# Two attention units a step: stacked queries, scores as 64-row products on both row tiles, low value products a step late

## The reference, cut to what matters

```python
x = x + tanh(g_xattn[0]) * attention(layernorm(x), ctx, ctx, 0, mask)   # the stage that changes
x = x + tanh(g_ffn[0]) * ffn(layernorm(x), ...)                          # unchanged here
# attention, f32: b=8, s=224, t=750, g=8 key/value heads, r=4 query heads each, d=64
scores = einsum('bsgrd,btgd->bgrst', xq, xk) / sqrt(64) + mask
probs  = softmax(scores, axis=-1)
out    = einsum('bgrst,btgd->bsgrd', probs, xv)
```

## Time and profile before

| what | value |
|---|---|
| time, median of 3 runs | 1172.92 us (1172.48 to 1173.42) |
| time of the profiled execution | 1173.51 us |
| its span, first to last instruction | 1171.7 us |
| granted TensorE clock | 1.00 of full speed throughout |
| first to last copy of transposed units (L742) | 20.3 to 879.9 us |
| busy PE, DVE, ACT, POOL | 1108.0, 1017.9, 897.6, 871.9 us |

### The profile page before, as it was taken

The page is one execution under the profiler, slowest core; times in us unless marked ns, Lnnn a source line. Parts: engine busy times, 40 slices in busy tenths (PEclk is TensorE's granted clock), DMA queues, the critical chain, the costliest instruction groups (busy, mean ns, idle before and its releaser), DMA issues.

```text
span 1171.7 us, 40472 instructions
## 1 busy us (share of the span) xinstructions
PE 1108.0 (95%) x17123; PEld 842.1 (72%) x17380; DVE 1017.9 (87%) x2325; ACT 897.6 (77%) x1162; POOL 871.9 (74%) x760
## 2 busy tenths in 40 slices
PE   4999999999999999999999999999999999999998
PEld 3777777777777777777777777777776655555554
DVE  6999999999999999999999999999984899676776
ACT  4898888888888888888888888888882443655544
POOL 6899999999988988898898889888892111333424
PEclk9999999999999999999999999999999999999999
DMA  9521331233114212412331132122126600002214
GB/s 327 153 70 42 67 115 43 54 77 98 42 49 111 77 42 60 114 49 55 70 105 42 48 72 54 42 60 51 49 81 188 239 1 1 1 36 109 102 79 180
DMA packets 102580, 95.44 MB, mean 81 GB/s; under 512 B 84481, under 2 KB 85505, under 8 KB 98562
## 3 DMA queue, kind: packets, MB, share of 16 engines
q1 hardware_dynamic: 101682, 91.79, 27.1%
q10 hardware_dynamic: 720, 1.05, 0.2%
HBM read 71.75 MB, written 20.97 MB: 79 GB/s over the span
## 4 chain that ended last, share of the span: by engine, by line
PE 79%; DVE 10%; issue 4%; POOL 3%; DMA 2%; ACT 1%; SPq 1%; DVEq 0%; POOLq 0%
PE psum L924 22%; PE psum L937 16%; PE psum L983 11%; PE psum L960 6%; PE psum L954 6%; PE psum L955 6%; DVE arena L1313 5%; DVE arena L1354 3%; PE psum L1061 3%; PE psum L902 2%; PE psum L970 2%; POOL arena L586 1%; PE psum L1100 1%; DMA arena<-in_k_t 1%; PE psum L996 1%
## 5 line engine op out<-in xcount | busy, mean ns | idle before, releaser
L586 POOL TENSOR_TENSOR arena<-arena 128x768 bf16<-128x768 f32 x448 | 651.2, 1470 | 72.6 <-ACT arena L742 71.6
L1313 DVE CUSTOM_DVE_ANT_0 arena<-psum,arena 128x750 f32<-128x750 f32 x448 | 419.3, 936 | 53.0 <-PE psum L924 45.9
L742 ACT ACTIVATE arena<-psum 128x768 f32<-128x768 f32 x448 | 362.9, 810 | 103.6 <-PE psum L937 103.5
L746 ACT ACTIVATE arena<-arena,neg_max 128x750 f32<-128x750 f32 x448 | 409.6, 914 | 4.2 <-DVE neg_max L1313 4.0
L924 PE MATMUL psum<-arena 128*128 128x238 bf16 (+1 forms) x1570 | 317.5, 318 | 38.6 <-issue 32.5
L937 PE MATMUL psum<-ident,arena 64*128 64x64 f32 x5376 | 263.5, 231 | 3.2 <-ACT arena L742 2.0
L924 PEld LDWEIGHTS psum<-arena 128*128 128x128 bf16 x1792 | 137.4, 97 | 144.4 <-issue 1.7
L937 PEld LDWEIGHTS psum<-ident,arena 64*128 64x128 f32 x5376 | 203.7, 138 | 38.8 <-issue 8.4
L954 PE MATMUL psum<-arena 128*128 128x65 bf16 (+1 forms) x2688 | 227.8, 195 | 0.0
L955 PE MATMUL psum<-arena 128*128 128x64 bf16 (+1 forms) x2688 | 226.7, 193 | 0.0
L954 PEld LDWEIGHTS psum<-arena 128*128 128x128 bf16 (+1 forms) x2688 | 198.6, 98 | 4.9 <-DVE arena L1354 0.2
(11 more groups left out here) (167 smaller groups left out, 1001.3 us busy)
## 6 DMA issues: line engine op xcount, KB each, us to landing
arena<-in_k_t SPq DMA_DIRECT2D x128, 187.5 KB, 3.2
arena<-in_v_rows SPq DMA_DIRECT2D x64, 192.0 KB, 2.9
out<-arena SPq DMA_DIRECT2D x10, 1024.0 KB, 3.9
arena<-in_x_top SPq DMA_DIRECT2D x8, 1024.0 KB, 5.3
arena<-in_x_rest SPq DMA_DIRECT2D x8, 768.0 KB, 4.6
spill<-arena SPq DMA_DIRECT2D x96, 64.0 KB, 2.3
arena<-spill SPq DMA_DIRECT2D x6, 1024.0 KB, 10.2
arena<-in_w_t SPq DMA_DIRECT2D x4, 1024.0 KB, 16.3
```

What stands on the lines that cost most here:

```text
L586: pool.tensor_tensor(p_lo[:, n % RING, :], p_sb[:, n % RING, :], high(p_sb[:, n % RING, :]), ALU.subtract).then_inc(p_split, 1)
L742: act.activation(p_sb[:, n % RING, :].rearrange("p (c h q) -> p h c q", h=2, q=HALF), turned_ps, ACT.Copy).then_inc(evac_a, 1)
L746: act.activation(s_sb[:, n % RING, 0:CTX], s_sb[:, n % RING, 0:CTX], ACT.Exp, bias=neg_max[:, n % 4, :], scale=-1.0).then_inc(exped, 1)
L1313: dve.tensor_tensor_reduce(s_sb[:, n % RING, 0:CTX], flat_ps[:, score_at(n):score_at(n) + CTX], mask_sb[:, max(n % UNITS - REP + 1, 0), :] ...
```

## The change

The kernel after works on two consecutive units in one step; a pair of groups (14 units) is 7 steps, and there are 224 steps.

- Scores: the stationary operands are `q_hi` and `q_lo`, with 64 rows for the first unit of the step and 64 for the second. Each matmul has 64 contraction rows, on row tile 0 for the first unit and on row tile 1 for the second, and the two are issued one behind the other. There are three products (high-high, low-high, high-low) in place of four. Both units of the step write banks 0 to 3, and the next step's scores wait until both were reduced.
- The units of the second group of a pair come in the order `SECOND`, so that the two units of a step always lie in the two row halves of one turned block.
- Low values move from DVE to POOL (`split_v`). The low probabilities of both units are one POOL instruction. The low value products of a step are issued in the next step.
- Queries: one high and one low instruction over 128 partitions in place of two each over 64.
- DVE does the two reductions of a step first and then the rest of that step; ACT does copy, exponential, copy, exponential.
- Rings of four; SP's list goes by pairs of groups: its order around `spill_rest` and the second `load_k` is new. The load of `wvu` now waits for the last scores.

```diff
-RING = 3
+RING = 4
...
+SECOND = (4, 0, 1, 2, 3, 5, 6)
...
+            for both in range(PAIRS):
+                b, at = both // 4, both % 4
+                if both + 1 < PAIRS:
+                    sp.wait_ge(scored, 2 * UNITS * both + UNITS + 1)
+                    load_k(2 * both + 2)
+                if both > 0:
+                    sp.wait_ge(valued, 2 * UNITS * both)
+                    load_v(2 * both + 1)
+                if at == 0 and b > 0:
                     spill_rest(b - 1)
...
+                if at == 0 and b + 1 < BATCH:
                     gather_rest(b + 1)
...
+                if at == 0 and b + 2 < BATCH:
+                    load_top(b + 2)
+                if both + 1 < PAIRS:
+                    sp.wait_ge(scored, 2 * UNITS * (both + 1))
+                    load_k(2 * both + 3)
...
+                if both + 1 < PAIRS:
+                    sp.wait_ge(valued, 2 * UNITS * both + UNITS)
+                    load_v(2 * both + 2)
...
+            for i in range(FIRST, NP):
+                both, p = place(i)
+                j = i + 1
+                if 0 <= j < NP:
+                    pool.wait_ge(evac_a, 2 * j + 2)
+                    if j >= 2:
+                        pool.wait_ge(valued, 2 * (j - 1))
+                    slots = slice(2 * j % RING, 2 * j % RING + 2)
+                    pool.tensor_tensor(p_lo[:, slots, :], p_sb[:, slots, :], high(p_sb[:, slots, :]), ALU.subtract).then_inc(p_split, 1)
...
+                if p == 1:
+                    split_v(2 * both + 1)
+                if both + 1 < PAIRS:
+                    if p == 1:
+                        split_k(2 * both + 2)
+                    if p == 4:
+                        split_k(2 * both + 3)
+                    if p == 5:
+                        split_v(2 * both + 2)
...
+            def copy_unit(n):
+                act.wait_ge(turned, n + 1)
+                if n >= RING and n % 2 == 0:
+                    act.wait_ge(p_split, n // 2 - 1)
...
+            for i in range(FIRST, NP):
+                both, p = place(i)
+                for s in range(2):
+                    if 0 <= i + 1 < NP:
+                        copy_unit(2 * (i + 1) + s)
+                    if 0 <= i + 2 < NP:
+                        exp_unit(2 * (i + 2) + s)
...
+                if both >= 0 and p == 4 and both + 2 < PAIRS:
+                    norm_top(both + 2)
+                later = both // 4 + 1
+                if both >= 0 and both % 4 == 3 and later < BATCH:
+                    if p == 0:
+                        norm_rest(later, 0)
+                        norm_rest(later, 1)
+                    if p == 1:
+                        norm_rest(later, 2)
...
+            def score_pair(j):
...
+                if j >= 1:
+                    pe.wait_ge(maxed, 2 * j)
                 for cols in (slice(0, MAIN), slice(MAIN, CTX)):
...
+                    for term in range(3):
+                        for s in range(2):
+                            rows = slice(HALF * s, HALF * s + HALF)
+                            u = groups[s] % 2
+                            q = q_lo if term == 1 else q_hi
+                            kk = k_lo[rows, u, cols] if term == 2 else high(k_raw[rows, u, cols])
+                            mm = pe.matmul(flat_ps[:, score_at(s) + cols.start:score_at(s) + cols.stop], q[rows, both % 2, p, :], kk,
+                                           start=(term == 0), stop=(term == 2))
+                mm.then_inc(scored, 2)
...
+            for i in range(FIRST, NP + 1):
+                both, p = place(i)
+                if 0 <= i + 1 < NP:
+                    turn_unit(2 * (i + 1))
+                if 0 <= i + 3 < NP:
+                    score_pair(i + 3)
+                if 0 <= i + 1 < NP:
+                    turn_unit(2 * (i + 1) + 1)
...
+                if i >= 1:
+                    value_low(i - 1)
+                if 0 <= i < NP:
+                    value_high(i)
...
+                if 0 <= both and both + 1 < PAIRS:
+                    if p == 2:
+                        turn_q(both + 1, 0)
+                    if p == 6:
+                        turn_q(both + 1, 1)
...
+                        if s == 1 and n >= RING:
+                            dve.wait_ge(turned, n - RING + 1)
+                        dve.tensor_tensor_reduce(s_sb[:, n % RING, 0:CTX], flat_ps[:, score_at(s):score_at(s) + CTX],
...
+                if both >= 1 and p == 0:
+                    add_part(2 * both - 1, range(0, 3) if both < PAIRS else range(UNITS))
+                if both >= 1 and p == 1:
+                    add_part(2 * both - 1, range(3, UNITS))
+                if p == 4:
+                    add_part(2 * both, range(0, 3))
+                if p == 5:
+                    add_part(2 * both, range(3, UNITS))
+                if both + 1 < PAIRS:
+                    if p == 2:
+                        split_q(both + 1, 0)
+                    if p == 6:
+                        split_q(both + 1, 1)
...
+                if p == 3 and both % 4 == 1 and both // 4 + 1 < BATCH:
+                    merge_top(both // 4 + 1)
+                    merge_rest(both // 4 + 1)
```

More of the change, by code:

```diff
@@ L336, in flamingo_block, with place, unit, part_turns @@
         block = ctx.enter_context(nc.Block())
[L338 to L353, removed]
-        FIRST_BANK = (1, 0, 1)
[L356 to L364, removed]
+        def place(i):
+            return divmod(i, UNITS)
+        def unit(n):
+            both, at = divmod(n, 2 * UNITS)
+            return (2 * both, at) if at < UNITS else (2 * both + 1, SECOND[at - UNITS])
+        FIRST_TURNS = (range(0, 2), range(2, 4), range(4, 7))
+        FIRST_BANK = (1, 0, 1)
+        def part_turns(part):
+            return range(0, 4) if part == 0 else range(4, 7)
+        def part_bank(part):
+            return 1 - part
+        def parts_split(both, part):
+            return 2 * both + 2 + part
+        ALL_PARTS = parts_split(PAIRS - 1, 1)
         def rows_of(t):
@@ L602, in _ @@
-                if window == GROUPS - 2 and m == 4:
+                if both < 0:
+                    continue
+                if p == 1:
[7 more added lines that the diff above has]
+                        split_v(2 * both + 2)
+                if both % 4 == 2 and both // 4 + 1 < BATCH:
+                    if p == 0:
+                        root(both // 4 + 2, whole)
+                    if p == 1:
+                        factors(both // 4 + 2, whole)
@@ L893, in turn_rows @@
[L893 to L901 removed]
+                    pe.wait_ge(rest_widened, NB)
@@ new lines, in value_high @@
+            def value_high(j):
+                for s in range(2):
+                    n = 2 * j + s
+                    g, m = unit(n)
+                    u = g % 2
+                    if n % UNITS == 0:
+                        pe.wait_ge(v_split, g + 1)
+                        if g >= 2:
+                            pe.wait_ge(x_added, g - 1)
+                        pe.wait_ge(q_split, min(g + 3, ALL_PARTS) if g else 2)
+                    pe.wait_ge(evac_a, n + 1)
+                    at = m * (D + 1)
+                    o = mix_ps[:, u, at:at + D + 1]
+                    fresh = s == 0 or n % UNITS == 0
+                    for c in range(NCH):
+                        rows = chunk_rows(c)
+                        hi = high(p_sb[0:rows, n % RING, c * 128:(c + 1) * 128])
+                        pe.matmul(o, hi, high(v_raw[0:rows, u, c, :]), start=(fresh and c == 0), stop=False, skip_group_check=True)
+                        pe.matmul(o[:, 0:D], hi, v_lo[0:rows, u, c, :], start=False, stop=False, skip_group_check=True)
@@ new lines, in value_low @@
+            def value_low(j):
+                pe.wait_ge(p_split, j + 1)
+                for s in range(2):
+                    n = 2 * j + s
+                    g, m = unit(n)
+                    at = m * (D + 1)
+                    for c in range(NCH):
+                        rows = chunk_rows(c)
+                        lo = p_lo[0:rows, n % RING, c * 128:(c + 1) * 128]
+                        mm = pe.matmul(mix_ps[:, g % 2, at:at + D + 1], lo, high(v_raw[0:rows, g % 2, c, :]), start=False, stop=(c == NCH - 1),
+                                       skip_group_check=True)
+                    mm.then_inc(valued, 1)
```

396 lines of the change are left out of this document (147 added, 249 removed).

## The result

The kernel after takes 1234.53 us (median of 4, 1229.31 to 1235.78), the kernel before 1173.17 on the same chip (1172.48 to 1173.70): a ratio of 1.052 [1.048, 1.055], so 5% slower. The prediction was 1144 (1106 to 1178), faster with a chance of 0.79. It was wrong, in sign too.

The account below looks back on a forecast made before the run. PE (95% busy, 79% of the chain) bounds, no engine having over 12% spare. Copies' stretch: 765 + 12 + 11 + 10 + 20 + 3.5, plus 7 reserve, 828.5 against 859.6; with 2 at the end, 1144 us (1106 to 1178).

Parts of the forecast that it names:

- The scores on two row tiles, 0.99: PE's score matmuls of both units overlap on two row tiles, taking 0.99 us a step where it was 1.32.
- Rivals 2 and 4: Scores' row tiles overlap incompletely, 1164 or 1177 us, chance 0.08; no overlap at 512 columns, 1320 us, chance 0.03.
- The 77%: Scores on PE: the Trainium skill's share of full overlap for four row tiles, making them 1.29 us, result 1177.
- A step of 3.23: PE's time for one step of two units: 3.23 us, against 3.66 before.
- Norm of the rest rows, 12: The rest rows' three units and their normalisation cost 1.23 + 0.53 us in seven pairs: 12 us.
- POOL's prices: POOL's instruction times: low values 0.79 us, low keys 1.40 start to start, joined low probabilities of two units 2.72.
- Rival 5: POOL at its old prices, keys 1.72 and values 1.22, 24.9 us a pair: 1176 us, chance 0.07.
- POOL's lumps with w1, 11: Weight table work on POOL, 2 x 1.00 us in eight pairs, delays them 1.5 us each: together 11.
- rival 1: The lumps hide: SP is early enough and POOL's lumps count half, 1105 us, chance 0.20.
- DVE's rest beside the next scores: DVE's other work runs beside the next step's scores, with 1.51 us of room; only merges exceed it, 3.5 us.
- rival 3: One pair of score banks decides: DVE's rest lies between scores and reductions, step 4.02 us, total 1231, chance 0.07.
- SP's order, 20: Spills ahead of the second key load delay POOL's low keys and low parts 3.3 us in six batches: 20 us.

Follow-up runs that it names:

- the barrier run: The good order with one 128-row, one-column matmul between the six score matmuls of the first unit and the six of the second: 1323.5 us.
- the good order: Kernel after, gather and rest rows' load before second key load, spills after value load, top rows one pair later, POOL's factors and roots in step 3: 1136.3 us.
- the filler: Kernel after with matmuls on unused PSUM columns (200 and 160 of 48 columns) keeping PE busy in its twelve stalls: 1225.5 us, ratio 1.045.

## Why the prediction was wrong, point by point

- **The scores on two row tiles, 0.99: right.** Measured 0.99, and the barrier run shows that it is the overlap. Rivals 2 and 4 fall. The 77% didn't apply.
- **A step of 3.23: 0.11 short.** 3.34. The second transposes are 0.09 late (1.58 for 1.49), which is nearly all of it: from the end of the copy (851.88 and 0.81, so 852.69) to their start at 852.84 are 0.15 us, where I had 0.04 to hand over. With turned blocks and norm a pair is 24.73 instead of 23.91: 26 us over 32 pairs, the largest error inside the quiet steps.
- **Norm of the rest rows, 12: right.** 1.14 and 0.44 in seven pairs, 11.
- **POOL's prices: right.** 1437 ns for low keys (1.40 start to start), 827 for low values (0.79 start to start), 2748 for the joined low part. Rival 5 falls.
- **POOL's lumps with w1, 11: nearly nothing.** The table in the good order has 24.78 against 24.73 us in two of these pairs and 25.29 in two others. The factors cost 1.2 in step 3 of the kernel after and, with the weight table in the same pair, 2.0: 11 us, 10 forecast. Of rival 1 this is the half that came true.
- **DVE's rest beside the next scores: right in its plain steps.** PE waits for L1355 in 6 steps only, those of stall 2, and the merges by themselves cost nothing (3.5 forecast). So rival 3, whose 1231 us is near the measured time, is right by accident: its mechanism, DVE's rest in every step, didn't occur.
- **SP's order, 20: this step failed.** The mechanism that I described (spills ahead of the second key load, POOL and then ACT late) was there, but sized for a landing of 3.2 us, and the load lands 6 us after issue behind the 1 MB of x, which stands in my own list of that queue. 36 instead of 20: 6.8 us a time in the five batches with that load, 2.4 in the one without, where I had 3.3 for all six.
- **What SP's order does to the rest rows: missing.** I had followed the spills and the keys through the new list, but not `load_rest`, whose place behind `spread` now meets a statistic in the same step as the merges. I counted 3.5 us of "merges" there as DVE's work. 48 us.
- **The start:** one wait of 4.2 us for the first keys of the next pair, which landed some 12 us after issue (28.6 to 40.4), 5 us with what follows it; I had put the start at 0. What delayed them wasn't looked into.
- **The clock: not considered.** The steps behind stall 1 are slower by 10 us (6 x 1.44, and twice some 0.6 in the next one); the filler gave back 9, net of some 6 that it cost.
- **The end: +2 forecast, +8 measured**, with a wait of 9.4 us for the root of the last statistics, which POOL makes behind its last low parts. With the root moved the end is 297.6 us against 291.8, so the root was only some 2 of it; the other 4 beyond the forecast I didn't trace.

Summed: 791 (32 pairs at 24.73) + 11 + 11 + 36 + 48 + 5 + 10 = 912, as measured, where I had 828.5. With SP's order written by need the same step gives 1136 and 1134 us, where I had 1144: without stalls it is faster by the quiet sum (815.6 against 828.5, since the SP term, the w1 lumps and the 7 us of reserve go and 26 come in). That this is so near my figure is in part luck, since terms of some 40 us too much and one of 26 us too little nearly cancel. PE is still the busiest engine (770 of 815.6 us), but with 58% of the chain, 31% being POOL's and ACT's, it is no longer the bound by itself; in the kernel after, SP's list decided.

## What to carry to other kernels

When a list of issues is rewritten, write down for every DMA in it the last step at which it is needed and the event that it waits for, and compare them with the step in which its user runs. A load that waits for a result and a user that stands directly behind that result in the same engine's list are a cycle that costs the issues in between and a landing each time, here 3.5 and 4 us. And take a landing time from a row where the same neighbours are in flight, not from the median of all.

## What the runs showed of the hardware

- Two 64-row matmuls on different row tiles overlap fully (twelve in 1.15 us), even where three of one tile stand in front of three of the other in the program; a one-column matmul of 128 rows between them ends it (six in 1.15 us).
- In the twelve stalls the granted clock went to 0.50 during a wait of PE of 2.4 to 7.4 us or within 1 us behind it, and stayed there for 6.8 or 10.2 us, once for 3.4. With matmuls filling the waits it was at 1.00 in most of them (19.2 us at 0.50 in all, where it was 106.7).
- A 375 KB pair of key loads landed some 3 us after issue with no large load in front and some 6 us after issue behind 1 MB on the same queue.
